# Two weight layers over eight batches on one core: the quarter products start at batch 3 instead of batch 2, and every engine's order of work is rewritten

## The reference

```python
x = x + (x @ W0.T + b0 + (x @ (2 * mask[b] - 1)) * coeff[b])       # layer 0, mask int32 1024x1024 per batch
x = x + (x @ W1.T + b1 + (x @ A[slot[b]]) @ Bm[slot[b]] * 2.0)      # layer 1, A 1024x16, Bm 16x1024 per batch
```

## Time and profile before

| what | value |
|---|---|
| median of 3 runs | 398.44 us (397.39 to 400.43) |
| profiled execution | 398.56 us |
| its span, first to last instruction | 395.9 us |
| PE busy, share of the span | 374.8 us, 95% |
| DVE busy | 312.2 us, 79% |
| ACT busy | 202.2 us, 51% |
| POOL busy | 108.2 us, 27% |
| mean granted clock of TensorE | 0.987 |

### The profile page before, as it was taken

One profiled execution on the slowest core, in us unless ns is written; L12 is line 12 of the kernel. 1 busy time (PEld: TensorE's weight loads), 2 busy tenths in 40 slices (PEclk: granted clock), 3 DMA queues, 4 the chain that ended last, 5 costly groups with the idle time before them and its releaser, 6 DMA issues.

```text
span 395.9 us, 5420 instructions
## 1 busy us (share of the span) xinstructions
PE 374.8 (95%) x1934; PEld 313.8 (79%) x1934; DVE 312.2 (79%) x364; ACT 202.2 (51%) x310; POOL 108.2 (27%) x128
## 2 busy tenths in 40 slices
PE   5999995989799998999999999999999999999996
PEld 5988874877588886888778887788878887788875
DVE  2997988568999899948899489948899379957623
ACT  3545854239356476606673267616673257515520
POOL 1234643644430733003400234002410124001300
PEclk9899998999989999999999999999999999999999
DMA  7999999997834998079941999069961999055002
GB/s 248 404 398 324 377 384 386 361 386 264 276 132 130 318 381 288 0 242 335 369 171 49 304 392 361 11 188 346 368 215 46 289 387 366 29 166 199 0 0 106
DMA packets 52075, 98.93 MB, mean 250 GB/s; under 512 B 3642, under 2 KB 12882, under 8 KB 52050
## 3 DMA queue, kind: packets, MB, share of 16 engines
q1 hardware_dynamic: 49104, 89.93, 66.3%
q10 hardware_dynamic: 2882, 8.66, 5.7%
q0 software_dynamic: 64, 0.01, 0.0%
HBM read 90.19 MB, written 8.39 MB: 249 GB/s over the span
## 4 chain that ended last, share of the span: by engine, by line
PE 56%; DMA 17%; DVE 13%; ACT 5%; SPq 3%; POOL 3%; issue 2%; ACTq 0%; DVEq 0%; POOLq 0%
PE bank L556 27%; PE bank L525 14%; DMA ring_raw<-in_mask 10%; PE bank L531 7%; DVE ring_raw L919 4%; DMA w_raw<-in_w 4%; PE bank L567 4%; ACT ring L688 3%; DVE ring L929 3%; DVE y_raw L987 2%; PE bank L597 2%; SPq L302 2%; DMA x_both<-in_x 2%; POOL ring_raw L393 2%; DMA ring_raw<-in_w 1%
## 5 line engine op out<-in xcount | busy, mean ns | idle before, releaser
L556 PE MATMUL bank<-w_two,y_two 128*128 128x512 f32 x696 | 166.1, 393 | 3.5 <-DVE y_two L1022 2.9
L556 PEld LDWEIGHTS bank<-w_two,y_two 128*128 128x128 f32 x696 | 129.7, 189 | 34.0 <-DVE y_two L1022 4.8
L688 ACT ACTIVATE ring<-ring_raw,coeff_neg 128x1024 fp32r<-128x1024 f32 (+1 forms) x67 | 74.3, 1113 | 129.9 <-DVE ring_raw L919 128.9
L525 PE MATMUL bank<-x_two,ring 128*128 128x512 f32 x448 | 128.1, 397 | 1.7 <-ACT ring L688 1.7
L919 DVE SCALAR_TENSOR_TENSOR ring_raw<-ring_raw,coeff_two 128x1024 f32<-128x1024 int32 (+1 forms) x67 | 84.7, 1276 | 42.7 <-DMA ring_raw<-in_mask 37.9
L929 DVE SCALAR_TENSOR_TENSOR ring<-ring_raw,coeff_neg,ring 128x1024 fp32r<-128x1024 f32 (+1 forms) x67 | 84.2, 1263 | 13.5 <-ACT ring L688 13.2
L525 PEld LDWEIGHTS bank<-x_two,ring 128*128 128x128 f32 x448 | 78.8, 190 | 13.7 <-issue 1.8
L393 POOL TENSOR_TENSOR ring_raw<-ring_raw,ident 128x128 f32<-128x128 f32 x56 | 40.2, 739 | 174.6 <-DMA ring_raw<-in_w 174.6
L531 PE MATMUL bank<-x_two,ring 128*128 128x256 f32 x448 | 78.6, 282 | 0.1
L531 PEld LDWEIGHTS bank<-x_two,ring 128*128 128x128 f32 x448 | 71.0, 190 | 9.1 <-DVE ring L929 0.8
L1022 DVE TENSOR_TENSOR y_two<-y_raw,y_two 128x512 fp32r<-128x512 f32 x42 | 33.9, 829 | 1.8 <-ACT y_two L736 1.3
(11 more groups left out here) (47 smaller groups left out, 216.6 us busy)
## 6 DMA issues: line engine op xcount, KB each, us to landing
ring_raw<-in_w SPq DMA_DIRECT2D x63, 512.0 KB, 8.3
ring_raw<-in_mask SPq DMA_DIRECT2D x63, 512.0 KB, 9.3
w_raw<-in_w SPq DMA_DIRECT2D x20, 512.0 KB, 12.4
x_both<-in_x SPq DMA_DIRECT2D x31, 256.0 KB, 5.4
out<-z_rows ACTq DMA_DIRECT2D x15, 512.0 KB, 7.5
b_raw<-in_lora_b SPq DMA_DIRECT2D x8, 448.0 KB, 3.7
ring_raw<-in_w SPq DMA_DIRECT2D x2, 256.0 KB, 4.5
ring_raw<-in_mask SPq DMA_DIRECT2D x2, 256.0 KB, 5.2
```

Source lines behind the costliest of these rows:

```text
L525: pe.matmul(layer0_bank(b, o)[:, 0:2 * T], w, x_two[:, k, :, :], start=(k == 0), stop=False, skip_group_check=True)
L556: ins = pe.matmul(bank[:], y_two[:, q, k, yp, :], w1_two[wp][:, j, k, :], start=(start and k == 0 and n == 0), stop=False, skip_group_chec ...
L688: act.activation(wc_hi[:, e % RING, lo:hi], sums[:, e % RING, lo:hi], ACT.Identity, bias=coeff_neg[:, b:b + 1]).then_inc(wc_hi_done, 1)
```

## The change

`FIRST` becomes 3: batch 2 gets plain products and its four z copies, and loses its `y_add`, `p_copy`, `p_add` and `z_add`. The T sums are made over batches 1 and 2, one half c in each (T3 at the end of batch 2); their loads stand behind the units 6 and 7 of these batches and behind the low-rank loads. Their diagonals go from POOL to DVE. W1 is loaded in one run, with the low-rank pair behind it. In batch 1 x is loaded before unit 0. POOL makes the bias pieces before the W1 diagonals. On ACT and DVE the order is written out anew for batches 1 and 2. For batches from 3 on, units 0 and 1 of the next batch are made after the last y part instead of before `y_sum(b, 4)`; x, the units 2 to 5 and `p_add` are interleaved in another way. x lies in SBUF by pairs, so that a load writes 2 KB runs instead of 1 KB, and the moving operand of a layer 0 matmul is two runs of 256 numbers with a gap of 1 KB instead of one run of 512.

The core of the diff. Of ACT's and DVE's lists only the lines of the new order are shown; the old order is in the functions above.

```diff
-    FIRST = 2
+    FIRST = 3
...
-        x_both = nc.alloc_sbuf_tensor_at("x_both", [P, KT, 2, T], F32, offset=x_at)
-        x_two = nc.alloc_sbuf_tensor_at("x_two", [P, KT, 2, T], F32R, offset=x_at)
-        x_raw = x_both[:, :, 1, :]
+        x_both = nc.alloc_sbuf_tensor_at("x_both", [P, XG, 2, PAIR, T], F32, offset=x_at)
+        x_two = nc.alloc_sbuf_tensor_at("x_two", [P, XG, 2, PAIR, T], F32R, offset=x_at)
+        x_raw = x_both[:, :, 1]
...
-                sp.dma_start(x_raw[:, PAIR * g:PAIR * (g + 1), :],
-                             x[b, g]).then_inc(x_in[g], 16)
+                sp.dma_start(x_raw[:, g], x[b, g]).then_inc(x_in[g], 16)
...
                 load_weights(0, k)
                 if k % PAIR == 1 and k < KT - 1:
                     load_x(0, k // PAIR + 1)
-            load_w1(0)
-            load_w1(1)
+            for k in range(KT):
+                load_w1(k)
             sp.wait_ge(ids_in, 16)
             load_lora(0)
-            for k in range(2, KT):
-                load_w1(k)
             for b in range(1, NB):
-                before = PAIR if b == 1 else HT
-                for u in range(before):
+                first = 0 if b == 1 else HT
+                for u in range(first):
                     load_weights(b, u)
                 for g in range(XG):
                     load_x(b, g)
-                for u in range(before, RING):
+                for u in range(first, RING):
                     load_weights(b, u)
                 if b == FIRST:
...
                     for c in range(2):
                         load_t(T3, c, 1, W22, t_in[T3, c])
                         load_t(T3, c, 0, W12, t_other_in[T3, c])
-                    load_lora(b)
-                if b == 1:
-
-                    for c in range(2):
-                        load_t(T1, c, 1, W12, t_in[T1, c])
-                        load_t(T1, c, 0, W11, t_other_in[T1, c])
-                        load_t(T2, c, 1, W22, t_in[T2, c])
-                        load_t(T4, c, 1, W21, t_in[T4, c])
-                    load_lora(b)
-                elif b > FIRST:
+                if b >= FIRST:
                     load_lora(b)
                 for u in range(RING, KT):
                     load_weights(b, u)
+                if b < FIRST:
+                    load_lora(b)
+
+                    load_t(T1, b - 1, 1, W12, t_in[T1, b - 1])
+                    load_t(T1, b - 1, 0, W11, t_other_in[T1, b - 1])
+                    load_t(T2, b - 1, 1, W22, t_in[T2, b - 1])
+                    load_t(T4, b - 1, 1, W21, t_in[T4, b - 1])
...
-            w1_diagonal(0)
-            w1_diagonal(1)
-            lora_a_diff(0)
-            for k in range(2, KT):
-                w1_diagonal(k)
-            lora_a_low(0)
-            pool.wait_ge(a_lo_done, 1)
+            pool.wait_ge(w0_diag, KT)
...
             pool.dma_start(b_stack[B_ALL + 1:B_ALL + 2, :], b1_parts[:, 1, :]).then_inc(b1_done, 16)
+            for k in range(KT):
+                w1_diagonal(k)
+            lora_a_diff(0)
+            lora_a_low(0)
             w0_diagonal(1, 0)
             w0_diagonal(1, 1)
             pool.wait_ge(w0_diag, diagonals(1, 1))
...
             lora_b_low(0, 1)
             for b in range(1, NB):
                 pool.wait_ge(b_lo_done, 2 * b)
-                if b == 1:
-                    for c in range(2):
-                        t_diagonal(T1, c)
-                        t_diagonal(T2, c)
-                elif b == FIRST:
-                    for c in range(2):
-                        t_diagonal(T3, c)
...
-                pe.matmul(layer0_bank(b, o)[:, 0:2 * T], w, x_two[:, k, :, :], start=(k == 0), stop=False,
+                pe.matmul(layer0_bank(b, o)[:, 0:2 * T], w, x_two[:, k // PAIR, :, k % PAIR, :], start=(k == 0), stop=False,
...
             w1_high(0)
             act.wait_ge(cols_in, 16)
             for g in range(XG):
                 y_high_first(g)
                 w1_high(g + 1)
+            for k in range(XG + 1, KT):
+                w1_high(k)
+            lora_a_high(0)
             lora_b_high(0)
             lora_b_copy(0, 0)
             for g in range(XG):
                 x_high(1, g)
+            weights_high(1, 0)
             lora_b_copy(0, 1)
+            weights_high(1, 1)
+            h_high(0)
             weights_high(1, 2)
             weights_high(1, 3)
             for i in range(4):
                 z_copy(0, i)
+            for u in range(HT, KT - 1):
+                weights_high(1, u)
             store(0, 0)
             store(0, 1)
+            for o in range(HT):
+                y_copy(1, o)
+            weights_high(1, KT - 1)
+            y_high_pair(1, 0)
+            y_high_pair(1, 1)
+            lora_b_high(1)
+            lora_b_copy(1, 0)
+            lora_a_high(1)
+            for o in range(HT, KT):
+                y_copy(1, o)
+            y_high_pair(1, 2)
+            y_high_pair(1, 3)
+            lora_b_copy(1, 1)
+            for u in range(3):
+                weights_high(2, u)
+            h_high(1)
+            weights_high(2, 3)
+            for g in range(XG):
+                x_high(2, g)
+            z_copy(1, 0)
+            weights_high(2, 4)
+            z_copy(1, 1)
+            weights_high(2, 5)
+            z_copy(1, 2)
+            t_high(T1, 0)
+            z_copy(1, 3)
+            t_high(T2, 0)
+            store(1, 0)
+            store(1, 1)
+            weights_high(2, KT - 2)
+            t_high(T4, 0)
+            for o in range(HT):
+                y_copy(2, o)
+            weights_high(2, KT - 1)
+            y_high_pair(2, 0)
+            y_high_pair(2, 1)
+            lora_b_high(2)
+            lora_b_copy(2, 0)
+            for o in range(HT, KT):
+                y_copy(2, o)
+            y_high_pair(2, 2)
+            y_high_pair(2, 3)
...
+            for b in range(FIRST, NB):
+                weights_high(b, KT - 2)
+                store(b - 1, 0)
+                store(b - 1, 1)
+                for o in range(HT):
+                    y_copy(b, o)
+                weights_high(b, KT - 1)
+                y_high(b, Y11)
+                y_high(b, S3)
                 lora_b_high(b)
                 lora_b_copy(b, 0)
+                lora_a_high(b)
+                for o in range(HT, KT):
+                    y_copy(b, o)
+                y_high(b, V12)
+                y_high(b, Y22)
+                lora_b_copy(b, 1)
+                p_copy(b, 0)
+                y_high(b, S1)
+                p_copy(b, 1)
+                y_high(b, S2)
+                y_high(b, S4)
                 if b + 1 < NB:
                     weights_high(b + 1, 0)
                     weights_high(b + 1, 1)
+                    x_high(b + 1, 0)
+                    x_high(b + 1, 1)
+                h_high(b)
+                if b + 1 < NB:
                     weights_high(b + 1, PAIR)
+                    x_high(b + 1, 2)
                     weights_high(b + 1, HT - 1)
+                    x_high(b + 1, 3)
+                p_copy(b, 2)
...
+            def t_diagonal(t, c):
+
+                if t == T1:
+                    dve.wait_ge(t_other_in[t, c], 16)
+                else:
+                    dve.wait_ge(t_in[t, c], 16)
+                for k in range(PAIR * c, PAIR * (c + 1)):
+                    blk = w1_raw[0 if t == T1 else 1][:, t, k, k * P:(k + 1) * P]
+                    ins = dve.tensor_tensor(blk, blk, ident[:], ALU.add)
+                ins.then_inc(t_diag, 1)
...
                 w1_low(k)
             x_low(1, 0)
             x_low(1, 1)
+            weights_sum(1, 0)
             x_low(1, 2)
             x_low(1, 3)
+            step(1, 0)
+            step(1, 1)
             h_low(0)
+            step(1, 2)
             step(1, 3)
+            step(1, 4)
+            weights_low(1, 5)
+            weights_sum(1, 6)
+            for o in range(HT):
+                y_sum(1, o)
+            weights_low(1, 6)
+            weights_sum(1, 7)
+            weights_low(1, 7)
+            y_low_pair(1, 0)
+            y_low_pair(1, 1)
+            weights_sum(2, 0)
+            for o in range(HT, KT):
+                y_sum(1, o)
+            weights_sum(2, 1)
+            y_low_pair(1, 2)
+            y_low_pair(1, 3)
+            weights_low(2, 0)
+            weights_sum(2, 2)
+            weights_low(2, 1)
+            weights_low(2, 2)
+            weights_sum(2, 3)
+            h_low(1)
+            for g in range(XG):
+                x_low(2, g)
+            weights_low(2, 3)
+            t_diagonal(T1, 0)
+            t_diagonal(T2, 0)
+            t_sub(T1, 0)
+            weights_sum(2, 4)
+            t_sub(T2, 0)
+            weights_low(2, 4)
+            weights_sum(2, 5)
+            t_sub(T4, 0)
+            weights_low(2, 5)
+            t_low(T1, 0)
+            t_low(T2, 0)
+            weights_sum(2, 6)
+            t_low(T4, 0)
+            weights_low(2, 6)
+            for o in range(HT):
```

(75 more changed lines are left out.)

203 lines of the change are left out of this document (31 added, 172 removed).

## The result

| | before | after |
|---|---|---|
| median, us | 398.01 (397.39 to 400.43, 4 runs) | 386.47 (385.81 to 387.0, 4 runs) |
| profiled execution, us | 398.56 | 386.49 |
| its span, us | 395.9 | 384.7 |

The ratio is 0.970 (95% interval 0.965 to 0.974). The prediction said 386.0, between 383.5 and 391.5. The total agrees to 0.5 us; the terms under it do not all, and some of their errors cancel.

A forecast was written before the change was run, and what follows sets the result against it. PE, busy 95% of the span, was taken as the bound. Span 395.9 less 15.95 us above clean times, plus 2.73 for matmuls and 0.5, gives 383.2; with 2.66 outside, 385.9, predicted as 386.0, range 383.5 to 391.5.

The forecast's parts named there:

- the stall near 129: Layer 0 of batch 2: PE would wait about 0.5 us near 129 for the weights of unit 7.
- no stall of PE above 1 us: Sign of being right: no PE wait above 1 us from its first matmul of layer 1 of batch 0 on.
- Close of batch 0 and what follows: Batch 0's close through batch 1's layer 0: the 4.21 us wait for h and 4.06 us excess with slow clock go.
- It starts at 84.6 ... with 3 us to spare: Layer 1 of batch 1: last y parts ready at 92.5, wanted at 95.5, so the 2.36 us stall goes.
- the second rival: T's halves delay batch 2's units by over 3 us; layer 1 of batch 1 stalls again: 389.9 us, chance 0.10.
- Layer 1 of batch 2: Layer 1 of batch 2 at 24.8 us, its 1.45 us wait gone, with DVE in time for batch 3's units.
- The start: Up to layer 1 of batch 0: x in 2 KB runs lands faster, gaining 0 to 0.8 us, taken as 0.
- Batches 3 to 7: Layer 1 from batch 3 on: y parts ahead of the next batch's units remove stalls, gaining 2.1 us.
- Quarter products from batch 3: Batch 2 with plain products: twelve more matmuls on PE cost 2.73 us, straight on the path.
- Split operand: Layer 0's moving operand in two runs costs nothing; the rival of 13.4 us more, 399.4, had chance 0.05.
- diagonals on DVE: T's diagonal steps on DVE: 0.22 us each, twelve making 2.6 us in DVE's idle time.
- Layer 0 of batch 2: `weights_high(2, 6)` ahead of `t_high(T4, 0)`, and stores ahead of unit 6, delay units 6 and 7: 0.5 us charged.

The follow-up runs named there:

- Experiment 10: Kernel before with the high and low split of batch 0's h one step earlier on ACT and DVE: 400.04 us, ratio 1.000 to before.
- experiment 3: Kernel after with all eight T1, T2, T4 loads ahead of units 6 and 7 of batch 1 again: 387.14 us, ratio 0.969 to before.
- Experiment 6: Kernel after with batch 1's second y half ahead of unit 0 of batch 2, and `lora_a_high(1)` behind it: 385.21 us, ratio 0.966 to before.
- Experiment 7: Kernel after with `h_low(2)` three steps earlier, ahead of the sum of unit 2 of batch 3: 385.43 us, ratio 0.968 to before.
- experiment 1: Kernel after with x in 1 KB runs again and the moving operand one run: 388.39 us, ratio 0.972 to before.
- experiment 9: Kernel before with x in 2 KB runs and nothing else: 397.32 us, ratio 0.996 to before.
- experiments 11: Kernel before with units 0 and 1 of the next batch behind the last y part, batches 2 to 6: 393.93 us, ratio 0.986 to before.
- experiment 12: Kernel before with quarter products only from batch 3 on, T3 loaded and made one batch later: 399.47 us, ratio 1.000 to before.
- experiment 8: Kernel after with early h of batch 2, batch 1's y ahead of units, and T4's first-half split behind units 6 and 7: 384.01 us, ratio 0.962 to before.

## Why the prediction was right, and where it was not

**By its own signs** the prediction passed on the clock (1.00 throughout), the close of batch 0, the stall near 129 (0.40 for 0.5) and the layers from batch 3 on. It failed on "no stall of PE above 1 us": there are two, 1.60 and 1.15, and layer 1 of batch 2 took 26.04 us instead of 24.8.

**Close of batch 0 and what follows: right, and sized right.** 8.27 predicted, 7.81 measured, clock 1.00 as said. Experiment 10 shows that this is one gain with two causes: h in time is worth nothing while unit 6 is late. There the sum of unit 6 came at 82.06, in the kernel after at 69.64. With the T loads ahead of the units but everything else new it came at 74.67 and cost three brackets of 1.43 us in all. So the place of the T loads is 5.0 us of those 12.4, and 7.4 belong to the rest: the earlier start (1.6), W1 in one run, the low-rank pair and z stores in other places. Which of these, no run separates, and the T loads were not moved alone in the kernel before.

**"It starts at 84.6 ... with 3 us to spare": the step that failed.** I had the loads of unit 0 landed by 86 and `lora_a_high(1)` done at 88. PE was a microsecond earlier than I thought (83.55) and wanted the last y parts at 94.6 instead of 95.5. The mask came at 87.8, POOL's diagonal of unit 1 ended at 90.1 and `lora_a_high(1)` at 90.76, and two y parts took 2.36 us beside POOL instead of 1.3, so that they were ready at 96.2 instead of 92.5. That is 0.9 and 3.7 off my 3 us to spare, and gives 1.60 us of bracket in place of none: the loads were put too early. It was the second rival's mechanism in small: in experiment 3, without the T loads in front, the sum of unit 0 came 2.1 us earlier. Experiment 6 shows that y ahead of the units and of `lora_a_high(1)` removes the wait, 1.6 us in the trace and 1.3 by the medians.

**Layer 1 of batch 2: not foreseen.** I wrote that DVE would be in time there and looked only at units 3 to 5, not at `h_low(2)`, which stands six unit steps and three T steps behind the last y part. `close` of the first result wants it at 151.8; it came at 152.46. Experiment 7 removes the wait (24.67 us for the layer).

**The start: right in kind, mis-sized.** I took 0 of a range of 0 to 0.8; it is 1.6 (trace), 1.9 (experiment 1), 1.6 (experiment 9, 0.2 to 3.0 by its interval). These pairs are at the upper end: layer 1 of batch 0 began at 35.84 to 36.35 in the nine traces with 2 KB runs, and at 37.47, 37.52, 37.56, 36.65 and 36.67 in the five with 1 KB runs, 1.0 apart in the mean. "Batch 0 is paced by weights behind it" was half wrong: PE's first product came 2.7 us earlier (7.34 for 10.06), of which waits for later operands took back 1.1. I had also overlooked a fall of the clock behind the first wait of PE for x in the kernel before. It costs nothing that shows: from PE's first product to layer 1 it is 27.41, 27.49 and 27.32 us in the three traces with such a fall (before, experiments 10 and 1), and 27.52 and 27.46 in the two 1 KB traces without (experiments 11 and 12).

```profile
10.06 1.22 PE L490 MATMUL bank<-x_two,ring 128*128 128x256 f32 x8 [3.33 <-DVE x_two L969]
...
10.06:15.06 5.00, 4.80 (x26) 4.59 (x27) 4.97 (x7) 2.58 (x4) 1.06 (x2) 0.68 1.02 406
```

**Batches 3 to 7: right, mis-sized.** 2.1 predicted, 2.77 between the two traces, 2.74 in experiment 11, and 3.95 undone in the new kernel. The old order's own layers vary from trace to trace (89.46 to 91.56 for the four), so the gain does, from 1.7 to 3.8. Two causes: the clean layer is 21.93, so I measured excess from a row that itself had 0.18; and brackets show only part of it.

**Quarter products from batch 3: right.** The 2.73 for twelve matmuls is seen in 24.65 in place of 21.93 (experiments 8, 11 and 12). With the order kept no cost can be told (-1.0 to +1.2 us by the interval), since the order's loss in batch 2 goes with it; with the order of experiment 11 it should be a plain loss of 2.7, which was not run. Whether batch 1 could carry all T work with the rest of the new order is open too.

**Split operand, diagonals on DVE: right** (a clean layer 0 takes 22.4 us in both layouts; 0.22 us each). **Layer 0 of batch 2:** 0.98 for 0.5, `t_high(T4, 0)` ahead of `y_copy`, as said; experiment 8 has 22.42 there.

**What cancelled.** In the span I missed by 1.5: +1.63 start, -0.46, -1.61, -0.48, -1.20, +0.67, -0.07. The start's 1.63, which I had put at nothing, hid the two waits: that is luck. The time outside the span went from 2.66 to 1.79, which I had left as it was, so the total is off by 0.5 only. That is luck too and no gain of the change: it is 1.74 to 2.91 in the 29 executions of the kernel before beside experiments 9 to 12, and 1.79 to 2.40 in the four of the kernel after. By stages of the two traces the kernel after is faster by h and unit 6 of batch 1 together with their clock (7.8 us), the order from batch 3 on (2.8), a shorter stall without a slow clock in layer 1 of batch 1 (2.3) and the 2 KB runs (1.6). It pays with 3.3 us in batch 2: the twelve matmuls (2.7), and new waits of 1.0 and 1.4, less the 1.8 that layer 1 of batch 2 had lost before.

## What to carry to other kernels

When a stall is removed, look for the next operand whose arrival is fixed by a queue and not by the engine that stalled: in experiment 10 one stall lost 3.7 us, the next grew by 3.0, the slow clock moved with it, and the time stayed. On an engine that takes its work in order, put what the next matmuls need ahead of what the next batch needs, and list small items such as h by their own due time. The excess of a stage over a clean one says more than its brackets, but the clean row must be the lowest of all that repeat. And a total that agrees does not vouch for its terms: check each against its own stage, in more than one trace.

## What the runs showed of the hardware

- **Landing of x by run length.** The same 256 KB issued at 1.17 to 1.19 us were taken up at 5.75 us in 2 KB runs and at 8.65 in 1 KB runs, beside weights on another queue (5.70 and 8.79 in the kernels of experiments 9 and 1). Over all fourteen traces it is 5.64 to 6.12 in 2 KB runs; in 1 KB runs it is 8.65, 8.66 and 8.79, but 7.72 and 7.80 in experiments 11 and 12:

```profile
7.72 0.63 ACT L705 ACTIVATE x_two<-x_both 128x512 fp32r<-128x512 f32 x1 [3.23 <-DMA x_both<-in_x]
```

The Trainium skill (DMA: Bandwidth & Descriptors, the table at its head) has full rate from 512 B on; by it the two should be alike. Here the 1 KB runs were 1.6 to 3.2 us later. The first sum of weights went the other way, 4.78 to 5.01 with 1 KB runs and 5.51 to 6.01 with 2 KB, which speaks for a division between the two queues; no run measures x alone.
- **The clock behind idle stretches.** It was 0.50 to 0.70 in the 5 us behind all ten brackets from 2.66 to 5.30 us in the fourteen traces, and behind 2.41 (twice), 2.37, 2.36 and 2.35. It stayed at 1.00 behind 2.17, 2.16, 1.67 and 1.60, and, in experiment 12, behind 2.42 (at 9.21) and 2.40:

```profile
105.08 2.04 PE L567 MATMUL bank<-y_two,a_parts 128*32 128x512 f32 x8 [2.40 <-DVE y_two L994]
...
105.00:110.00 5.00, 4.92 (x22) 3.49 (x23) 4.98 (x5) 2.63 (x4) 2.35 (x1) 1.00 0.00 0
```

So at about 2.4 us both were seen; what decides there is open. The lower value is the lower of the clock's two levels. The cost shows in two traces of the same order: layer 1 of batch 1 takes 28.78 us with a fall behind 2.36, and 27.20 without one behind 2.40, so the fall costs 1.6. In layer 0 of batch 1 of experiment 10 it is 29.99 - 22.43 - 4.69 = 2.87. Each is more than half of its stall.
- **Steps beside POOL.** A 1024-column DVE step of 1.28 us took 2.30 beside a POOL instruction (146.60), two y parts 2.36 instead of 1.29, and two POOL diagonals 3.14 instead of 0.88 (138.09). Moving the T diagonals back to POOL changed no total that can be told, but these single steps lie ahead of both brackets that were not foreseen. That they would have been shorter alone is read from the same steps elsewhere in the trace, not tested.
